# Queries, picks and group 0's scores of a fused attention kernel moved in among the last experts, the identity products of the attention groups taken out

## The chip, the cores and the metric

The kernel runs on one NeuronCore of a Trainium2 chip. The metric is device time in microseconds (us) of one execution, lower is better. The kernel before takes 216.92 us, the median of 3 runs (216.85 to 217.7).

## The reference

Input are `x` and a context, both 4 batches x 256 tokens x 128 features, in fp32. Two layers follow each other.

- Layer 0, attention: a normalised `x` against the context (similarities with softmax both ways), concatenated and sent through a linear layer, added to `x`.
- Layer 0, experts: after a second layer norm, `out = sum over 8 experts of weight[e] * ((silu(x W1[e]) * (x W2[e])) W3[e])`, hidden size 256, with the weights a softmax over the top 2 of 8 logits. All 8 experts are computed for all tokens; added to `x`.
- Layer 1, attention: third layer norm, then for 16 heads of size 8: `Q = x Wq`, `K = ctx Wk`, `V = ctx Wv`, `softmax(Q K^T / sqrt(8)) V`, then `Wo` and a bias; added to `x`.
- Layer 1, last product: fourth layer norm, values rounded to 8-bit floats, one 128x128 product, a bias, added to `x`.

## The kernel before, in words

Each engine has its own instruction stream, written out by hand in one `nc.Block`; there is no planner. An engine executes its stream in order, and semaphores (`S[...]`) tie the streams together. TensorE (`pe`) writes into eight PSUM banks `bk[0]` to `bk[7]`; ScalarE (`act`) and VectorE (`dve`) read them; GpSimd (`pool`) works on SBUF only. 1024 tokens are 8 tiles of 128, or two halves of 512.

**Start (to about 38.6 us).** First attention and values. `project_keys` (L1056) makes the keys of both halves in banks 2 and 3 after `turn("ln2", ...)`; ScalarE copies them over `ctxT` (L402), rounds them to `kx` (L488), and GpSimd makes the low part (L280).

**Experts.** 16 units `n`: half `n // 8`, expert `n % 8`. `up(n)` (L1084) makes four 128x512 results in banks 0 to 3, each of three products in a fast fp32 format (high and low parts, L933 to L935). ScalarE's `gates` (L404) applies silu, VectorE's `hidden` (L751) multiplies. `down(n - 2)` (L1101, products at L1110) follows `up(n)` on TensorE, into bank 4 or 5; VectorE's `weigh` (L760) adds the result times the expert's weight to `xs` (four instructions at L768). Once half 0 is done, at unit 9, VectorE takes the third norm's moments of it (`sum_moments`), GpSimd makes the deviation, ScalarE scales in units 10 and 11 (`third_scaled`), TensorE turns after `down(10)` in unit 12 (`turn("ln3", ..., 6, 0)`), projects the queries ahead of `up(13)`, and makes the picks of groups 0 and 1 ahead of `up(14)` and `up(15)`.

**Attention groups.** 16 groups `m`: batch `b = m // 4` and four heads `g = m % 4`. For a group:
- `pick_group` (L1120) lays queries and keys of four heads out on four quadrants of 32 rows by a selection matrix (bank 0 or 7), and ScalarE's `stacked` copies them to `stk`.
- `scores(m, r)`, r = 0 to 3 (L1132): one head each, 2 products; VectorE's `maxima` (L783, reduction at L789) takes the negated row maximum.
- `turn_maxima(m)` (L1149) turns the maxima, VectorE's `shifted` (L794) adds them to the queries as one more row (`qa`), and `shifted_scores(m)` (L1156, into banks 3 to 6) makes the shifted scores, of which ScalarE's `exps` (L442) are the probabilities.
- `outputs(m)` (L1170) multiplies with the values; `o_copy` saves them.
- After a batch: `turn_outputs(b, t)`, `normalise(b, t)` (VectorE, L802), `turn_normalised(b)`, ScalarE's copy, `output_layer(b)`, and `add_attention(b)` (VectorE, L812).

`pe_group(m)` (L1242) sets the order on TensorE: `turn_maxima(m)`; `bank7_used(m)` (the products for other batches that go through bank 7, and here the turn of the third norm's half 1 at m = 3 and the projection of its queries at m = 4); `scores(m+1, 1)`; `pick_group(m+3)`; `shifted_scores(m)`; `scores(m+1, 2)` and `(m+1, 3)`; `bank7_free(m)` (waits until bank 7 may be written); `outputs(m-1)`; `scores(m+2, 0)`. `keep_warm(bank, count)` (L945) multiplies the identity by itself `count` times; nothing reads the result. It appears 23 times between unit 15 and group 11 (each product is two records in the trace, L947). VectorE's order is in `dve_group` (L819), ScalarE's in `act_group` (L460).

**End.** After group 15's outputs: batch 3's turns, output layer, fourth norm, rounding, last product, in three chunks.

Of the kernel before, what the change touches and what calls it, by code (L numbers as in the profile page):

```python
# [33 lines left out]
WARMED = (0, 1, 2, 2 * G - 1, 3 * G - 1)  # L34
# [12 lines left out]
def build(nc, x_d, ctx_d, ctxT_d, small_d, wc_d, const_d, wl_d, bl_d, wg_d, w12_d, w3_d,  # L47
# [9 lines left out]
    with stack:  # L57
# [84 lines left out]
        x3T = sb("x3T", [P, TOK])  # L142
        qx = sb("qx", [P, 2, TOK], r32)
# [82 lines left out]
        def _(pool):  # L226
# [53 lines left out]
            pool.tensor_tensor(kx[:, 1, :], ctxT[:, :], plain(kx[:, 0, :]), ALU.subtract).then_inc(S["k_lo"], 1)  # L280
# [36 lines left out]
        def _(act):  # L317
# [78 lines left out]

            values_out(0)
            values_out(1)
            normed_hi(0)
            for h in range(2):  # L400
                act.wait_ge(S["k_ps"], h + 1)
                act.copy(ctxT[:, h * HALF:(h + 1) * HALF], bk[2 + h][:, :]).then_inc(S["k_out"], 1)  # L402
# [53 lines left out]
            def turned_out(b):  # L456
                act.wait_ge(S["aoT_ps"], b + 1)
                act.copy(aoT[:, :], bk[7][:, 0:SEQ]).then_inc(S["aoT_ev"], 1)

            def act_group(m):  # L460
# [5 lines left out]
                if m in TURNED_AT:  # L466
                    turned_out(b - 1)
                exps(m, 0)
                exps(m, 1)
                if m >= 1:  # L470
                    o_copy(m - 1, 0 if m == GROUPS - 1 else 7)
                if m + 3 < GROUPS:
                    stacked(m + 3)
                if m == 2:
                    for t in range(*HALVES[1]):
                        third_scaled(t)


            for n in range(UNITS):
                if n == 4:  # L480
                    logits_out(1)
                if n == UNITS - 3:
                    queries_hi(0)
                if n >= UNITS - 2:
                    stacked(n - UNITS + 2, 7)
                gates(n, n == 0)
                if n == 2:
                    act.copy(kx[:, 0, :], ctxT[:, :]).then_inc(S["k_hi"], 1)  # L488
# [13 lines left out]
            stacked(2)  # L502
# [53 lines left out]
        def _(dve):  # L556
# [203 lines left out]
            def weigh(n):  # L760
# [5 lines left out]
                for t in range(TPH):  # L766
                    tile = h * TPH + t
                    ins = dve.scalar_tensor_tensor(xs[:, tile, :], bk[4 + n % 2][:, t * P:(t + 1) * P],  # L768
# [43 lines left out]
            def add_attention(b, tiles):  # L812
# [3 lines left out]
                                  bk[7][:, 0:SEQ].rearrange("p (t d) -> p t d", t=TPB), ALU.add)\  # L816
                    .then_inc(S["x3_s"], 1)

            def dve_group(m):  # L819
# [5 lines left out]
                if more:  # L825
                    maxima(m + 1, 1)
                if m == G:
# [9 lines left out]
                if m in (0, 1):  # L837
                    sum_moments((TPH + TPB * m, TPH + TPB * (m + 1)))
                if b == BATCH - 1 and g == 1:
                    normalise(b - 1, 1)  # L840
                if more:
                    maxima(m + 1, 3)
                if m == GROUPS - 1:
                    moments(4, CHUNKS[0], lambda t: dve.wait_ge(S["x3_s"], t // TPB + 1))
                    add_attention(b - 1, slice(TPB * (b - 1), TPB * b))


            for n in range(UNITS):
# [7 lines left out]
                if n == UNITS - 3:  # L856
                    queries_lo(0)
                if n >= 2:
                    weigh(n - 2)
                if n == E + 1:  # L860
                    sum_moments(HALVES[0])
            weigh(UNITS - 2)
            dve.wait_ge(S["setup"], 1)
            maxima(0, 0, 1)
            weigh(UNITS - 1)
            maxima(0, 2, 3)
# [63 lines left out]
        def _(pe):  # L930
# [71 lines left out]
            context_to_query(1)  # L1002
            pe.wait_ge(S["cv_s"], 1)
# [52 lines left out]
            def project_keys(h):  # L1056
                if h == 0:
                    pe.wait_ge(S["aT_ev2"], BATCH - 1)
                ins = pe.matmul(bk[2 + h][:, :], wk[:, :], ctxT[:, h * HALF:(h + 1) * HALF], start=True, stop=True)
                ins.then_inc(S["k_ps"], 1)  # L1060

            for h in range(2):
                project_keys(h)
# [37 lines left out]
            def down(n):  # L1101
                e, p = n % E, n % 2
# [288 lines left out]
```

## Time and profile before

| | us |
|---|---|
| median of 3 runs | 216.92 |
| the profiled execution | 218.05 |
| its span (first to last instruction) | 216.3 |
| TensorE busy | 188.8 |
| VectorE busy | 139.3 |
| ScalarE busy | 103.9 |
| GpSimd busy | 36.7 |
| share of the chain that ended last: TensorE / VectorE / ScalarE | 74% / 11% / 5% |

The profile is one execution. Times in it are us from the span's start. PE is TensorE's products, PEld its weight loads, DVE VectorE, ACT ScalarE, POOL GpSimd. An fp32 product appears as two records. A product's end is modelled, and products are pipelined, so the step from one start to the next tells more than a duration. The granted clock is a share of 2.4 GHz; 0.50 is 1.2 GHz.

### The profile page before, as it was taken

The page shows a single profiled execution, that of the slowest core. Times are in us where ns is not written, and L with a number is a line of the kernel's source. Part 1 is how long each engine was busy: PE and PEld are TensorE (multiplying, and loading weights), DVE is VectorE, ACT ScalarE, POOL GpSimd, SP SyncE. Part 2 cuts the span into 40 slices and gives each one's busy share as a digit, 9 for nine tenths or more (in the row PEclk, how much of TensorE's full clock was granted, in tenths as well). Part 3 has the DMA queues.
Part 4 walks back from the last instruction along what each step waited for, and adds up shares of the span by engine and source line. Part 5 has one row for each costly group of instructions (what it writes and reads, how often), then busy time and mean ns, then how long its engine had stood idle before and what let it go on. Part 6 is the DMA issues. An engine that isn't in the chain of part 4 may idle for free.

```text
span 216.3 us, 3877 instructions
## 1 busy us (share of the span) xinstructions
PE 188.8 (87%) x1386; PEld 146.3 (68%) x1386; DVE 139.3 (64%) x404; ACT 103.9 (48%) x184; POOL 36.7 (17%) x52
## 2 busy tenths in 40 slices
PE   5599799999999999998999999799999998789221
PEld 4289498779798888996789886456666665554110
DVE  2559758666467647553546778477777876554684
ACT  2247467535422232533233146887577666345333
POOL 3623374624000000300000005200000000003400
PEclk9999999999999999999999999999999999655955
DMA  6992000000000000000000000000000000000002
GB/s 205 387 397 92 5 0 2 0 3 0 0 5 0 0 0 3 0 0 0 3 0 0 2 3 0 0 3 0 5 0 3 0 5 0 0 3 2 0 0 97
DMA packets 3330, 6.61 MB, mean 31 GB/s; under 512 B 880, under 2 KB 2160, under 8 KB 3056
## 3 DMA queue, kind: packets, MB, share of 16 engines
q1 hardware_dynamic: 1440, 5.51, 6.7%
q10 hardware_dynamic: 1872, 0.87, 1.4%
q8 instruction: 11, 0.18, 0.3%
q14 instruction: 7, 0.06, 0.1%
HBM read 5.84 MB, written 0.52 MB: 29 GB/s over the span
## 4 chain that ended last, share of the span: by engine, by line
PE 74%; DVE 11%; issue 5%; ACT 5%; ACTq 3%; POOL 1%; DVEq 0%
PE banks L1110 13%; PE bank L1144 9%; PE bank L1177 8%; PE bank L933 5%; PE bank L935 5%; PE bank L934 5%; DVE negm L789 4%; PE bank L947 3%; PE bank L1152 3%; PE banks L934 2%; PE banks L933 2%; PE banks L935 2%; ACTq L328 2%; PE bank L1186 2%; PE bank L1127 2%
## 5 line engine op out<-in xcount | busy, mean ns | idle before, releaser
L789 DVE TENSOR_REDUCE negm<-bank 128x2 f32<-128x512 f32 x64 | 43.0, 689 | 18.9 <-PE bank L1144 18.7
L446 ACT ACTIVATE raw<-banks 128x1024 f32<-128x1024 f32 x32 | 31.0, 1021 | 21.4 <-PE banks L1164 21.4
L409 ACT ACTIVATE att<-bank 128x512 f32<-128x512 f32 x32 | 19.1, 598 | 38.5 <-PE bank L935 25.6
L1144 PE MATMUL bank<-stk 32*128 32x256 f32 x128 | 29.9, 319 | 3.9 <-DVE negm L789 3.3
L1144 PEld LDWEIGHTS bank<-stk 32*128 32x128 f32 x128 | 19.4, 191 | 15.9 <-issue 12.8
L768 DVE SCALAR_TENSOR_TENSOR xs<-banks,rw,xs 128x128 f32<-128x128 f32 x64 | 18.0, 345 | 6.0 <-PE banks L1110 5.8
L1110 PEld LDWEIGHTS banks<-raw,attT 128*128 128x128 f32 x176 | 21.3, 191 | 0.9
L1110 PE MATMUL banks<-raw,attT 128*128 128x128 f32 x176 | 21.5, 275 | 0.0
L1177 PE MATMUL bank<-raw,vones 128*32 128x256 f32 x256 | 19.9, 433 | 1.1 <-DVE ao L808 1.0
L933 PE MATMUL bank<-xT,w 128*128 128x512 f32 x48 | 20.6, 428 | 0.0
L237 POOL TENSOR_SCALAR vpe<-mv 128x4 f32<-128x4 f32 (+1 forms) x9 | 2.4, 266 | 97.7 <-DVE mv L566 97.6
L935 PE MATMUL bank<-xT,w 128*128 128x512 f32 x48 | 18.8, 392 | 0.0
L934 PE MATMUL bank<-xT,w 128*128 128x512 f32 x48 | 18.8, 391 | 0.0
L438 ACT ACTIVATE stk<-bank,const 128x512 fp32r<-128x512 f32 x16 | 11.2, 699 | 8.8 <-PE bank L1127 8.8
L756 DVE TENSOR_TENSOR attT<-att,bank 128x512 f32<-128x512 f32 x11 | 7.5, 683 | 10.3 <-ACT att L409 10.3
L1164 PE MATMUL banks<-qa,stk 32*128 32x256 f32 x128 | 13.5, 335 | 0.5 <-DVE qa L798 0.5
L1177 PEld LDWEIGHTS bank<-raw,vones 128*32 128x32 f32 x256 | 8.4, 119 | 6.8 <-issue 1.9
L756 DVE TENSOR_TENSOR attT<-att,banks 128x512 f32<-128x512 f32 x11 | 7.6, 688 | 7.2 <-ACT att L409 7.2
L263 POOL TENSOR_TENSOR w<-raw,w 128x512 fp32r<-128x512 f32 x8 | 10.1, 1286 | 6.6 <-ACT w L341 5.2
L933 PEld LDWEIGHTS bank<-xT,w 128*128 128x128 f32 x48 | 9.0, 188 | 2.7 <-DVE xT L697 0.5
L1164 PEld LDWEIGHTS banks<-qa,stk 32*128 32x128 f32 x128 | 10.0, 198 | 0.9 <-DVE qa L798 0.9
L935 PEld LDWEIGHTS bank<-xT,w 128*128 128x128 f32 x48 | 9.0, 188 | 2.1
(194 smaller groups left out, 347.6 us busy)
## 6 DMA issues: line engine op xcount, KB each, us to landing
raw<-in_w SPq DMA_DIRECT2D x1, 2048.0 KB, 10.7
raw<-in_w SPq DMA_DIRECT2D x1, 1024.0 KB, 8.5
xs<-in_x SPq DMA_DIRECT2D x2, 256.0 KB, 3.2
ctxT<-in_ctxT SPq DMA_DIRECT2D x1, 512.0 KB, 5.3
ctx<-in_ctx SPq DMA_DIRECT2D x1, 512.0 KB, 7.4
wl<-in_wl SPq DMA_DIRECT2D x1, 256.0 KB, 7.6
picks<-in_sel ACTq DMA_DIRECT2D x1, 256.0 KB, 10.9
out<-cT SPq DMA_DIRECT2D x1, 256.0 KB, 2.1
```

What stands on the lines that cost most here:

```text
L409: act.activation(silus[:, k, :], bk[2 * k][:, :], ACT.Silu).then_inc(S["silu_s"], 1)
L446: act.activation(probs[:, m % 2, 2 * r:2 * r + 2, :, :].rearrange("p h k q -> p (h k q)"), pair[r][:, :], ACT.Exp, scale=ATT_SCALE).then_i ...
L756: dve.tensor_tensor(hid[n % 3][:, k, :], silus[:, k, :], bk[2 * k + 1][:, :], ALU.mult)\
L768: ins = dve.scalar_tensor_tensor(xs[:, tile, :], bk[4 + n % 2][:, t * P:(t + 1) * P], rw[:, tile, e:e + 1], xs[:, tile, :], ALU.mult, ALU.add)
L789: dve.tensor_reduce(negm[:, m % 2, :, c0:c0 + 1].rearrange("p t c -> p (t c)"), bk[score_bank(m, r)][:, :].rearrange("p (t k) -> p t k", t ...
L933: pe.matmul(out, w[0], x[0], start=start, stop=False)
L934: pe.matmul(out, w[0], x[1], start=False, stop=False)
L935: return pe.matmul(out, w[1], x[0], start=False, stop=stop)
L1110: ins = pe.matmul(bk[4 + p][:, rows], hid[n % 3][:, k, rows], w3raw[:, e, k * P:(k + 1) * P], start=t == 0 and k == 0, stop=t == TPH - 1 a ...
L1144: ins = pe.matmul(bk[score_bank(m, r)][:, t * SEQ:(t + 1) * SEQ], stk[rows, m % G, t * P:(t + 1) * P], stk[rows, m % G, SEQ:2 * SEQ], star ...
L1164: ins = pe.matmul(bk[3 + j][:, t * SEQ:(t + 1) * SEQ], stk[rows, g, SEQ + t * P:SEQ + (t + 1) * P], qa[rows, m % 2, :], start=True, stop=T ...
L1177: ins = pe.matmul(bk[bank][QUAD * j:QUAD * (j + 1), SEQ:2 * SEQ], vones[:, t, (m % G) * HPG + j, :], probs[:, m % 2, j, t, :], start=t == ...
```

## The change

- **Keys.** `project_keys(0)` moves up, to before the wait for `cv` (after `context_to_query(1)`), behind a wait for all attention DMAs; `project_keys(1)` stays after `turn("ln2", ...)`. ScalarE copies them to `kraw`, which is `x3T`'s memory, instead of `ctxT`, the first of them ahead of the values' copies.
- **Third norm, half 0, and queries.** All four scalings in unit 10, the turn in unit 11 after `up(11)`, the projection in unit 12 after `up(12)`, VectorE's `queries_lo` in unit 12.
- **Picks and group 0's scores.** Picks of groups 0, 1, 2 after `up(13)`, `up(14)`, `up(15)`; group 0's four scores around `down(12)` and `down(13)` in units 14 and 15, all through bank 6, and VectorE's reductions of them around `weigh(12)` and `weigh(13)`.
- **Last two downs.** `down(14)` goes to bank 0 after `scores(1, 0)`; `down(15)` goes to bank 7 inside group 0, after `shifted_scores(0)`. VectorE's `weigh(14)` and `weigh(15)` stand inside its group 0, each ahead of a reduction. `pick_group(3)` moves behind `scores(1, 2)`.
- **Third norm, half 1.** All four tiles' moments in group 1 (before: two in group 0, two in group 1); ScalarE's scalings ahead of `exps(2, ...)` (before: behind them).
- **Batch 2's outputs.** Both halves turned through bank 0: the first in group 13, the second at the end of group 13 (before: both at its start, one through bank 7, with `outputs(12)` waiting for both). `turn_normalised(2)` in group 14 and `output_layer(2)` at that group's end use bank 0. `add_attention(2)` moves from the end of VectorE's group 15 to the end of group 14. `outputs(14)` uses bank 7 and doesn't wait for `output_layer(2)`.
- **Identity products.** All 23 between unit 15 and group 11 go; four are added in group 15, behind `outputs(14)`. Those of the start stay.

The diff, cut to its core:

```diff
@@ placement of banks
         def score_bank(m, r):
             if m == 0:
-                return 2 - r % 2
+                return 6
...
         def turn_bank(b, t):
-            return 0 if t == 0 and b >= BATCH - 2 else 7
+            return 0 if b == BATCH - 2 or (t == 0 and b == BATCH - 1) else 7
+
+        def layer_bank(b):
+            return 0 if b == BATCH - 2 else 7
+
+        def y_bank(n):
+            return {UNITS - 2: 0, UNITS - 1: 7}.get(n, 4 + n % 2)
@@ ScalarE
+            keys_out(0)
             values_out(0)
             values_out(1)
             normed_hi(0)
...
+            keys_out(1)
...
+                if m == 2:
+                    for t in range(*HALVES[1]):
+                        third_scaled(t)
                 exps(m, 0)
                 exps(m, 1)
...
-                if m == 2:
-                    for t in range(*HALVES[1]):
-                        third_scaled(t)
...
-                if n == UNITS - 3:
+                gates(n, n == 0)
+                if n == UNITS - 4:
                     queries_hi(0)
-                if n >= UNITS - 2:
-                    stacked(n - UNITS + 2, 7)
-                gates(n, n == 0)
+                if n >= UNITS - 3:
+                    stacked(n - UNITS + 3, 7)
...
-                if n in (E + 2, E + 3):
-                    for k in range(HB):
-                        third_scaled(HB * (n - E - 2) + k)
-                if n == E + 4:
+                if n == E + 2:
+                    for t in range(*HALVES[0]):
+                        third_scaled(t)
+                if n == E + 3:
                     third_turned(0, TPH, 6, 0)
@@ VectorE, dve_group and units
                 if more:
                     maxima(m + 1, 1)
+                if m == 0:
+                    weigh(UNITS - 2)
...
                 if more:
                     maxima(m + 1, 2)
-                if m in (0, 1):
-                    sum_moments((TPH + TPB * m, TPH + TPB * (m + 1)))
+                if m == 0:
+                    weigh(UNITS - 1)
+                if m == 1:
+                    sum_moments(HALVES[1])
+                if more:
+                    maxima(m + 1, 3)
                 if b == BATCH - 1 and g == 1:
                     normalise(b - 1, 1)
-                if more:
-                    maxima(m + 1, 3)
+                if m == GROUPS - 2:
+                    add_attention(b - 1, slice(TPB * (b - 1), TPB * b))
...
+                if n >= UNITS - 2:
+                    maxima(0, 2 * (n - UNITS + 2))
                 if n >= 2:
                     weigh(n - 2)
+                if n >= UNITS - 2:
+                    maxima(0, 2 * (n - UNITS + 2) + 1)
@@ TensorE
+            pe.wait_ge(S["ld_att"], 7 * 16)
+            project_keys(0)
             pe.wait_ge(S["cv_s"], 1)
...
-                if m in WARMED:
-                    keep_warm(7, 2)
...
             def bank7_free(m):
                 b, g = m // G, m % G
+                if m == 1:
+                    pe.wait_ge(S["y_w"], UNITS)
...
-                if b >= 1 and g == 1:
-                    pe.wait_ge(S["ao_s"], TPB * (b - 1) + (1 if b < BATCH - 1 else TPB))
+                if 1 <= b < BATCH - 1 and g == 1:
+                    pe.wait_ge(S["ao_s"], TPB * (b - 1) + 1)
...
-                if m + 3 < GROUPS:
+                if 0 < m < GROUPS - 3:
                     pick_group(m + 3)
                 shifted_scores(m)
-                if final:
-                    pe.wait_ge(S["o_ev"], m - 1)
-                    output_layer(BATCH - 2)
-                    outputs(m - 1, 0)
+                if m == 0:
+                    down(UNITS - 1)
                 if more:
                     scores(m + 1, 2)
                     if m == 0:
-                        keep_warm(7, 2)
+                        pick_group(3)
                     scores(m + 1, 3)
-                if m == 0:
-                    keep_warm(7, 4)
-                if m >= 1 and not final:
+                if m >= 1:
                     bank7_free(m)
                     outputs(m - 1)
                 if m + 2 < GROUPS:
                     scores(m + 2, 0)
+                if m == 3 * G + 1:
+                    pe.wait_ge(S["ao_s"], TPB * (BATCH - 2) + 1)
+                    turn_outputs(BATCH - 2, 1)
+                if m == 3 * G + 2:
+                    pe.wait_ge(S["aoT_ev"], BATCH - 1)
+                    output_layer(BATCH - 2)
+                if final:
+                    keep_warm(2, 4)
...
-                if n == UNITS - 3:
-                    pe.wait_ge(S["route_s"], 18)
-                    project_queries(0)
-                if n == UNITS - 2:
-                    pe.wait_ge(S["pick_s"], 1)
-                    pe.wait_ge(S["k_lo"], 1)
-                if n >= UNITS - 2:
-                    pick_group(n - UNITS + 2, 7)
                 up(n)
...
+                if n == UNITS - 5:
+                    turn("ln3", "x3T_ps", 6, 0)
+                if n == UNITS - 4:
+                    pe.wait_ge(S["route_s"], 18)
+                    project_queries(0)
+                if n == UNITS - 3:
+                    pe.wait_ge(S["pick_s"], 1)
+                    pe.wait_ge(S["k_lo"], 1)
+                if n >= UNITS - 3:
+                    pick_group(n - UNITS + 3, 7)
+                if n >= UNITS - 2:
+                    scores(0, 2 * (n - UNITS + 2))
                 down(n - 2)
...
+                if n >= UNITS - 2:
+                    scores(0, 2 * (n - UNITS + 2) + 1)
+            pe.wait_ge(S["hid_s"], HB * UNITS)
+            scores(1, 0)
             down(UNITS - 2)
-            pe.wait_ge(S["hid_s"], HB * UNITS)
-            for r in range(2):
-                scores(0, r)
-            down(UNITS - 1)
-            pick_group(2)
-            scores(0, 2)
-            pe.wait_ge(S["stack_s"], 2)
-            keep_warm(7, 4)
-            scores(0, 3)
-            keep_warm(7, 3)
-            scores(1, 0)
```

## Rows read from the trace of the kernel before

**Rows 1.** The page, granted TensorE clock in 40 slices, in tenths.

```profile
PEclk9999999999999999999999999999999999655955
```

**Rows 2.** Windows: stretch, length, busy us (records) by engine, clock, DMA share, GB/s.

```profile
113.53:127.87 14.34, 14.28 (x115) 12.43 (x113) 10.26 (x27) 5.29 (x7) 0.00 (x0) 1.00 0.01 2
127.87:142.02 14.15, 12.47 (x128) 8.28 (x127) 9.64 (x19) 9.88 (x16) 4.28 (x6) 1.00 0.00 1
...
180.15:186.65 6.50, 4.50 (x44) 2.88 (x43) 3.82 (x9) 3.01 (x5) 0.22 (x1) 0.92 0.00 0
186.65:199.21 12.56, 11.24 (x81) 6.16 (x81) 6.81 (x24) 5.42 (x9) 2.29 (x4) 0.50 0.01 2
```

**Rows 3.** Timeline: start, us, instruction [idle before]; turn_maxima of groups 1, 3, 12 to 15.

```profile
127.87 0.44 PE L1152 MATMUL bank<-const,negm 128*128 128x128 f32 x2
...
136.15 0.44 PE L1152 MATMUL bank<-const,negm 128*128 128x128 f32 x2
...
176.01 0.44 PE L1152 MATMUL bank<-const,negm 128*128 128x128 f32 x2
...
180.15 0.44 PE L1152 MATMUL bank<-const,negm 128*128 128x128 f32 x2
...
186.65 0.69 PE L1152 MATMUL bank<-const,negm 128*128 128x128 f32 x2
...
191.94 0.69 PE L1152 MATMUL bank<-const,negm 128*128 128x128 f32 x2
```

**Rows 4.** Timeline: the wait for cv, and the start of unit 0.

```profile
23.98 0.31 PEld L1005 LDWEIGHTS banks<-const,cv 128*4 128x4 f32 x4 [1.71 <-DVE cv L638]
...
38.64 0.19 PEld L933 LDWEIGHTS bank<-xT,w 128*128 128x128 f32 x1 [0.51 <-DVE xT L697]
```

**Rows 5.** Timeline of TensorE: turns, projection, first pick, and down(13).

```profile
97.14 0.60 PE L941 MATMUL banks<-const,xn 128*128 128x128 f32 x4
98.50 1.10 PE L1117 MATMUL bank<-x3T,wq 128*128 128x512 f32 x2 [0.77 <-ACT x3T L427]
...
104.61 0.47 PE L1127 MATMUL bank<-qx,pick 32*128 32x256 f32 x2 [0.46 <-DVE qx L779]
...
113.53 1.95 PE L1110 MATMUL banks<-raw,attT 128*128 128x128 f32 x16
```

**Rows 6.** Chain that ended last: start, us, what; down(15), identity products, scores.

```profile
117.69 1.98 PE banks L1110 x16
...
120.58 1.09 PE bank L947 x8
121.67 0.43 PE bank L1144 x2
```

**Rows 7.** Groups by line: count | busy, mean ns | idle before.

```profile
L789 DVE TENSOR_REDUCE negm<-bank 128x2 f32<-128x512 f32 x64 | 43.0, 689 | 18.9 <-PE bank L1144 18.7
...
L768 DVE SCALAR_TENSOR_TENSOR xs<-banks,rw,xs 128x128 f32<-128x128 f32 x64 | 18.0, 345 | 6.0 <-PE banks L1110 5.8
```

**Rows 8.** Timeline: third norm of half 1, and the scores behind its turn.

```profile
133.26 0.20 POOL L276 TENSOR_TENSOR nmr<-nmr,rstd 128x4 f32<-128x4 f32 x1
...
137.49 1.38 PE L941 MATMUL bank<-const,xn 128*128 128x128 f32 x4 [0.90 <-ACT xn L413]
...
138.79 0.38 PE L1144 MATMUL bank<-stk 32*128 32x256 f32 x1
```

**Rows 9.** Timeline: outputs of group 12, of groups 14 and 15, last turns.

```profile
184.80 1.19 PE L1177 MATMUL bank<-raw,vones 128*32 128x256 f32 x16 [1.02 <-DVE ao L808]
...
195.03 3.66 PE L1177 MATMUL bank<-raw,vones 128*32 128x256 f32 x32
...
199.21 1.13 PE L1186 MATMUL bank<-const,heads_out 128*128 128x128 f32 x8 [0.52 <-ACT heads_out L454]
```

**Rows 10.** Windows, columns as in rows 2: two stretches of 3.40 us.

```profile
134.90:138.30 3.40, 2.45 (x23) 1.21 (x15) 1.67 (x4) 3.40 (x8) 0.00 (x0) 1.00 0.00 0
182.20:185.60 3.40, 1.75 (x30) 1.07 (x26) 2.80 (x7) 1.94 (x2) 0.00 (x0) 1.00 0.00 0
```

More of the change, by code:

```diff
@@ L142, in build @@
         x3T = sb("x3T", [P, TOK])
+        kraw = x3T
         qx = sb("qx", [P, 2, TOK], r32)
@@ L395, in normed_hi, with keys_out @@
                 act.copy(xT[:, 0, h * HALF:(h + 1) * HALF], bk[4 + h][:, :]).then_inc(S["xT_hi"], 1)
+            def keys_out(h):
+                act.wait_ge(S["k_ps"], h + 1)
+                act.copy(kraw[:, h * HALF:(h + 1) * HALF], bk[2 + h][:, :]).then_inc(S["k_out"], 1)
+            keys_out(0)
             values_out(0)
@@ L399, in _ @@
             normed_hi(0)
-            for h in range(2):
-                act.wait_ge(S["k_ps"], h + 1)
-                act.copy(ctxT[:, h * HALF:(h + 1) * HALF], bk[2 + h][:, :]).then_inc(S["k_out"], 1)
+            keys_out(1)
             def gates(n, first):
@@ L457, in turned_out @@
                 act.wait_ge(S["aoT_ps"], b + 1)
-                act.copy(aoT[:, :], bk[7][:, 0:SEQ]).then_inc(S["aoT_ev"], 1)
+                act.copy(aoT[:, :], bk[layer_bank(b)][:, 0:SEQ]).then_inc(S["aoT_ev"], 1)
             def act_group(m):
@@ L855, in _ @@
                     routing(n // 5)
-                if n == UNITS - 3:
+                if n == UNITS - 4:
                     queries_lo(0)
+                if n == UNITS - 2:
+                    dve.wait_ge(S["setup"], 1)
+                if n >= UNITS - 2:
+                    maxima(0, 2 * (n - UNITS + 2))
                 if n >= 2:
                     weigh(n - 2)
+                if n >= UNITS - 2:
+                    maxima(0, 2 * (n - UNITS + 2) + 1)
                 if n == E + 1:
                     sum_moments(HALVES[0])
[L862 to L866, printed above, removed]
             for m in range(GROUPS):
@@ L1002, in _, with project_keys @@
             context_to_query(1)
+            def project_keys(h):
+                ins = pe.matmul(bk[2 + h][:, :], wk[:, :], ctxT[:, h * HALF:(h + 1) * HALF], start=True, stop=True)
+                ins.then_inc(S["k_ps"], 1)
+            pe.wait_ge(S["ld_att"], 7 * 16)
+            project_keys(0)
             pe.wait_ge(S["cv_s"], 1)
@@ L1054, in _ @@
             turn("ln2", "xT_ps", 4, 0)
[L1056 to L1063, printed above, removed]
+            project_keys(1)
             def logits(h):
@@ L1109, in down @@
                     for k in range(HB):
-                        ins = pe.matmul(bk[4 + p][:, rows], hid[n % 3][:, k, rows], w3raw[:, e, k * P:(k + 1) * P],
+                        ins = pe.matmul(bk[y_bank(n)][:, rows], hid[n % 3][:, k, rows], w3raw[:, e, k * P:(k + 1) * P],
                                         start=t == 0 and k == 0, stop=t == TPH - 1 and k == HB - 1)
@@ L1123, in pick_group @@
                 pe.wait_ge(S["stack_s"], m)
+                if m == 3:
+                    pe.wait_ge(S["y_w"], UNITS - 1)
                 cols, rows = slice(b * SEQ, (b + 1) * SEQ), slice(g * QUAD, (g + 1) * QUAD)
@@ L1133, in scores @@
                 pe.wait_ge(S["stack_s"], m + 1)
-                if r == 0 and m > 0:
+                if m == 0:
+                    pe.wait_ge(S["s1_max"], r)
+                elif r == 0:
                     pe.wait_ge(S["s1_max"], 4 * m - 1)
-                elif r == 2 and m > 0:
+                elif r == 2:
                     pe.wait_ge(S["qa_s"], m)
-                elif r == 3 or (r == 1 and m > 0):
+                else:
                     pe.wait_ge(S["s1_max"], 4 * m + (r + 1) // 2)
-                elif r == 2:
-                    pe.wait_ge(S["s1_max"], 1)
                 rows = slice(QUAD * r, QUAD * (r + 1))
@@ L1157, in shifted_scores @@
                 pe.wait_ge(S["qa_s"], m + 1)
+                if m == 0:
+                    pe.wait_ge(S["y_w"], UNITS - 2)
                 g = m % G
@@ L1192, in turn_normalised @@
                 for t in range(TPB):
-                    ins = pe.transpose(bk[7][:, t * P:(t + 1) * P], ao[:, t, :], ident)
+                    ins = pe.transpose(bk[layer_bank(b)][:, t * P:(t + 1) * P], ao[:, t, :], ident)
                 ins.then_inc(S["aoT_ps"], 1)
```

40 lines of the change are left out of this document (18 added, 22 removed).

## The prediction

> **What bounds the kernel now.** The page's chain and its slices come first. TensorE carries most of the chain (74% of the span on the page), and it runs at 2.4 GHz (granted clock 9 of 10 or more) until slice 34, falls to 1.2 GHz (5) for two slices and again at the very end [rows 1]. So instructions on TensorE's path are what counts, and waits in its queue. The stretches [rows 2] show where it isn't dense: from 127.87 to 142.02 it is busy 12.47 of 14.15 us, in group 13 (180.15 to 186.65) 4.50 of 6.50, and from 186.65 to 199.21 it works at 1.2 GHz. Then I read the rows of the places that the diff touches: the start, units 12 to 15, groups 0 to 3, groups 13 to 15.
>
> I write T(m) for the start of group m's `turn_maxima`; before, T(1) is 127.87, and a regular group takes 4.14 (176.01 to 180.15) [rows 3]. I lay the new order out instruction by instruction in this profile's times.
>
> **Keys earlier, at the start: 0.** `project_keys(0)` goes into TensorE's wait for `cv` (1.71 us idle before 23.98), and it takes about 0.9. Its new wait is for all 7 attention DMAs, behind which `cv`'s products and all that follow are queued; nearly no DMA moves after slice 3, so it should be met. Unit 0 starts when VectorE has written `xT` (0.51 us idle before 38.64) [rows 4], and neither the values nor the norm ahead of it move, so the second key product isn't on the path before nor after. ScalarE's first key copy falls where it waits for the values. Bounds: -0.5 (that idle) to +1 (should the DMAs be late); I take 0.
>
> **Units 11 to 15.** Turn, projection, picks of groups 0 and 1 are still issued before unit 15's last up product, one unit earlier each. What goes is two waits: TensorE idles from 97.59 to 98.50 for the copy of x3T (the four turns end 0.45 after 97.14) and from 103.99 to 104.61 for q's low part [rows 5], together 1.53. Now each product has a whole unit (4.5 us) between it and its use. On ScalarE the four scalings of group 0's norm come together, 1.65 to 1.75, in a gap of about 3 between two units' gates; VectorE's `queries_lo` delays `weigh(10)` by 0.7, which has over 2 of slack. Added before the end of up(15) are scores(0,0) and (0,1), 0.43 each [rows 6]. So `down(13)` could start at 113.53 - 1.53 + 0.86 = 112.86; but pick(2) (0.66) and scores(0,2) (0.43) now stand ahead of it.
>
> **From there to T(1).** TensorE: pick(2), scores(0,2), down(13) 1.78, scores(0,3), scores(1,0), down(14), 5.5 in all (a down of 16 products is 1.98 with the gap behind it, 1.78 where nothing stands between, scores 0.43 [rows 6]), so T(0) = 118.4. VectorE keeps up: its reductions (0.69) and weighings (four of 345 ns, overlapped to 1.13 together) [rows 7] end with maxima(0,3) at 117.75. Then turn 0.45, scores(1,1), VectorE's qa from about 118.95 to 119.36, shifted scores to 120.05, down(15) to 121.85, scores(1,2) to 122.28. Here VectorE becomes the bound: maxima(1,2) 122.4 to 123.1, weigh(15) to 124.2, maxima(1,3) to 124.9, and `turn_maxima(1)` waits for the last. TensorE has pick(3), scores(1,3), scores(2,0) until 123.8 and stands 1.25. T(1) = 125.05, gain 2.8. Of the 15 identity products (30 records) in this stretch, 4.1 us at 1.09 for four [rows 6], and the 1.53 of idle, only half comes back: the scores beside the experts had cheap cover for their reductions, but two weighings have moved behind. Bounds: 1.25 less if the weighing's wait is doubled, 4.1 if it is hidden: 1.5 to 4.1.
>
> **Groups 1 to 3.** All four tiles' moments now stand in group 1, 1.1 us instead of about 0.65, before maxima(2,3), so T(2) comes 4.45 after T(1), not 4.13: -0.3, and T(2) = 129.5. The deviation then takes GpSimd 2.13 (moments' end to nmr at 133.46), ready at 130.8. The scalings move ahead of exps(2): 130.85 to 132.5, exps(2) to 134.45 (0.8 later than it could), the heads' copy to 134.8. In group 3 the turn into bank 7 waits for that copy, 0.8 idle, but then finds its four tiles ready, 0.45, where it now waits 0.90 and is paced by ScalarE to 138.79 (1.38 busy from 137.49) [rows 8]. T(3) to scores(4,1) shrinks from 2.64 (136.15 [rows 3] to 138.79) to 1.7: +0.9. Bounds: 0 (exps(2) on the path by its whole 1.65) to 1.35.
>
> **Identity products in groups 7 and 11.** They stand between turn_maxima and scores(m+1,1), which has to wait for VectorE's reduction (0.69) anyway, so they are nearly covered: those groups take 4.34 and 4.32 against 4.14, and I take 0.4 for both (bounds 0 and 1.1, their whole length). Those of groups 0 to 2 are in the sum above or covered likewise. T(13) = 180.15 - 2.8 + 0.3 - 0.9 - 0.4 = 176.35.
>
> **Group 13.** Now it takes 6.50, since outputs(12) at 184.80 waits for both halves of `normalise(2)`, through bank 7 (1.02 idle before it) [rows 9]. After, turns and normalised values use bank 0, outputs(12) waits for nothing of theirs, and the second half is turned after scores(15,0). Added up: to the first turn 0.8, turn 0.53, scores(14,1) and its reduction to 2.55, scores(14,3) to 3.15, outputs 1.05, scores 0.43, second turn 0.45: T(14) = T(13) + 5.05, gain 1.45. The price is in group 14: maxima(15,0) is behind normalise(2,1) on VectorE, so scores(15,1) starts at +1.55, not +0.95, and the output layer (0.45) comes before T(15); 4.9 in all at full clock, against 5.29 now at half (186.65 to 191.94): gain 0.4.
>
> **Group 15.** Before, from T(15) at 191.94 to the last turns at 199.21 are 7.27: output layer, and 32 records of outputs in 3.66 at 1.2 GHz, started late [rows 9]. After: turn 0.44, qa by +1.05, shifted scores to +1.7, exps 1.94 to +3.8; outputs(14) and four identity products lie beside the exps; outputs(15) 1.1, copy 0.4: +5.5, gain 1.8. VectorE and GpSimd end chunk 0's norm at about +5.2, so they're just in time. From 199.21 to the end (216.3) nothing changes: 17.1.
>
> **The clock.** It falls at 185.65, after TensorE was busy 1.75 of the 3.40 us before, and comes back at 199.3; the loosest stretch without a fall is busy 2.45 of 3.40 [rows 10]. The new group 13 is as dense as a regular one (outputs, scores, turns in a row), so I take it at 2.4 GHz throughout; the gain of groups 14 and 15 (2.2) hangs on that, and partly on outputs at 1.02 instead of 1.89. The products that go are real ones. By the Trainium skill (TensorE: Matmul & The Clock Gate, Part 4: PE-mode transpose) a transpose doesn't count as TensorE work in the same way; by that rule stretches of turns would look emptier once identity products are out, and the clock might fall there; that would be rival A or, if it lasts, C. The row of 134.90 to 138.30, half of it turns with no identity product in it and a clock of 1.00, speaks against.
>
> **Sum.** 2.8 - 0.3 + 0.9 + 0.4 + 1.45 + 0.4 + 1.8 = 7.45. Span 216.3 - 7.4 = 208.9. The profiled execution took 218.05, 1.75 more than its span, so 210.65 for one like it; the median of the runs shown (216.92) lies 1.13 below the profiled one, so **209.5**.
>
> **Rivals.**
> A: the new wait before turn_maxima(1) drops the clock. There TensorE would be busy about 2.1 of 3.40 us, between the two cases of [rows 10]. Were it low for the same 13.6 us as before, three groups would take up to 5.29 instead of 4.14: +3.5, 213.0. For: the gap of 1.25 itself. Against: down(15), dense, stands just ahead. 15%.
> B: the fall in the last groups stays. The order of group 13 gains its 1.45, but groups 14 and 15 run at 1.2 GHz and pay the added reduction wait as well: gain 2.8 - 0.3 + 0.9 + 0.4 + 1.45 - 0.9 = 4.35, 212.6. For: group 14 has two gaps of 0.3 to 0.5. Against: the long outputs between. 12%.
> C, the other side: without its identity products the group loop doesn't hold the clock at all; once low at group 1, it stays. Each group then costs 1.15 more, and with 14 of them the time is 209.5 + 16 = 225.5; from the seventh low group on the change is slower than before (7 times 1.15 is over 7.4). For: every identity product in the loop goes. Against: groups 3 to 6 and 8 to 10 have none now, and hold 1.00 [rows 1]. 6% slower, 3% near break-even.
> D: the change doesn't do what it says at the crossing: VectorE's weighings and reductions take back all that the identity products gave (T(1) gains 0.5, not 2.8), 211.8. 8%.
>
> **Chances.** The forecast 56% (its own range 208.0 to 211.2), A 15, B 12, D 8, C 9. Within 0.5% is about what a measurement here can tell from no change. Faster 0.91, same 0.03, slower 0.06. The range reaches below for a crossing at its better bound (1.3) and up over A: 207.5 to 213.6.
>
> **What would show it.** Right: an idle of 1 to 1.5 before turn_maxima(1), T(1) near 125; about 0.8 of idle before the turn of x3T in group 3; group 13 near 5; granted clock 1.00 up to the last outputs, and these in 1.0 to 1.1 for 16; no idle over 0.2 before picks and projections in units 11 to 15. Wrong: a clock of 0.50 in any group, a wait for the DMAs before `project_keys(0)`, T(1) later than 126.5, or VectorE later than TensorE in each group rather than at the crossing alone.

## The result, and the profile after

The changed kernel takes 229.16 us (median of 4 runs, 227.68 to 229.99), the kernel before 217.17 in the same comparison (4 runs, 216.85 to 217.7): 1.054 times as long, 95% interval 1.048 to 1.060. I had forecast 209.5. A kernel that may or may not lose TensorE's clock has runs far apart, so the medians below are over all runs, with the lowest and the highest beside them, while a ratio with an interval compares only the runs of each kernel within 1.5% of its fastest. The loss is one thing, TensorE's clock. Here are the page's slices (one digit for 5.6 us):

```profile
PEclk9889999999999999999999655555555599979655
```

It falls in slice 23 (6) and is at 5, 1.2 GHz, in the nine slices behind it; [rows 1] had 9 there. The windows of the changed kernel (columns as in [rows 2]) are the stretch up to the fall, the low stretch, and two regular groups after it:

```profile
121.80:125.20 3.40, 1.81 (x21) 1.39 (x20) 3.10 (x7) 0.50 (x1) 0.00 (x0) 1.00 0.01 2
127.82:179.20 51.38, 51.05 (x330) 32.80 (x329) 26.22 (x48) 26.37 (x40) 4.01 (x7) 0.50 0.00 1
183.68:191.96 8.28, 7.68 (x83) 5.26 (x82) 6.25 (x11) 6.17 (x10) 0.17 (x1) 1.00 0.01 3
```

In the 3.40 us before the fall TensorE is busy 1.81, as little as before the old kernel's fall (1.75, [rows 10]). Then it is busy 51.05 of 51.38 us and still the level doesn't come back before about 180.1. The starts of `turn_maxima` (timeline, L1169; they answer to [rows 3]):

```profile
122.90 0.44 PE L1169 MATMUL bank<-const,negm 128*128 128x128 f32 x2 [1.07 <-DVE negm L797]
...
127.82 0.69 PE L1169 MATMUL bank<-const,negm 128*128 128x128 f32 x2
...
153.87 0.69 PE L1169 MATMUL bank<-const,negm 128*128 128x128 f32 x2
...
160.31 0.69 PE L1169 MATMUL bank<-const,negm 128*128 128x128 f32 x2
...
187.82 0.44 PE L1169 MATMUL bank<-const,negm 128*128 128x128 f32 x2
...
191.96 0.44 PE L1169 MATMUL bank<-const,negm 128*128 128x128 f32 x2
...
197.04 0.38 PE L1169 MATMUL bank<-const,negm 128*128 128x128 f32 x2
...
202.97 0.64 PE L1169 MATMUL bank<-const,negm 128*128 128x128 f32 x2
```

The first of them is T(1), with the new wait of 1.07. A regular group at the low level takes 6.44 (153.87 to 160.31), at the high one 4.14 (187.82 to 191.96): 2.30 more each. From T(1) to T(13), 122.90 to 191.96, are 69.06; in the best variant below (experiment 10), which holds the clock there, the same stretch takes 51.07. So the long low stretch costs about 18.0. The start of the kernel looks as forecast: keys and then `cv`, unit 0 waiting for `xT`:

```profile
21.26 1.02 PE L1018 MATMUL bank<-ctxT,wk 128*128 128x512 f32 x2
22.74 0.31 PEld L1025 LDWEIGHTS banks<-const,cv 128*4 128x4 f32 x4 [1.28 <-DVE cv L646]
...
37.41 0.50 PE L947 MATMUL bank<-xT,w 128*128 128x512 f32 x1 [0.54 <-DVE xT L705]
```

All of that lies 1.2 us earlier than in the profile before, already ahead of the keys. From unit 0 to T(1) are 85.49 us, before 89.23 (38.64 in [rows 4] to 127.87).

### The profile page after: what moved, and what is told of

Its sections match the earlier page's. It is cut to its first block, busy times and chain, and to the rows that moved or that the text cites. A ratio compares the mean times of both kernels' runs of the same rounds, so it can differ in the third digit from the quotient of the medians.

```text
span 225.9 us, 3803 instructions
## 1 busy us (share of the span) xinstructions
PE 201.4 (89%) x1348; PEld 152.1 (67%) x1348; DVE 141.2 (63%) x404; ACT 104.2 (46%) x184; POOL 37.0 (16%) x52
## 4 chain that ended last, share of the span: by engine, by line
PE 75%; DVE 12%; issue 4%; ACT 4%; ACTq 3%; POOL 1%; DVEq 0%
PE bank L1161 12%; PE banks L1125 11%; PE bank L1196 10%; PE bank L947 5%; PE bank L949 5%; PE bank L948 5%; PE banks L1183 3%; PE bank L1169 3%; DVE negm L797 2%; PE bank L1205 2%; PE banks L947 2%; PE banks L948 2%; PE banks L949 2%; PE bank L1125 2%; PE bank L1218 2%
## 5 line engine op out<-in xcount | busy, mean ns | idle before, releaser
L797 DVE TENSOR_REDUCE negm<-bank 128x2 f32<-128x512 f32 x60 | 40.2, 689 | 31.7 <-PE bank L1161 31.6
L1161 PE MATMUL bank<-stk 32*128 32x256 f32 x120 | 35.2, 397 | 3.2 <-DVE negm L797 2.8
L1161 PEld LDWEIGHTS bank<-stk 32*128 32x128 f32 x120 | 24.1, 253 | 19.6 <-issue 18.8
L1196 PE MATMUL bank<-raw,vones 128*32 128x256 f32 x256 | 25.7, 534 | 0.0
L776 DVE SCALAR_TENSOR_TENSOR xs<-banks,rw,xs 128x128 f32<-128x128 f32 x56 | 15.8, 344 | 7.8 <-PE banks L1125 7.7
L1125 PEld LDWEIGHTS banks<-raw,attT 128*128 128x128 f32 x160 | 19.2, 192 | 1.2 <-issue 0.5
L1125 PE MATMUL banks<-raw,attT 128*128 128x128 f32 x160 | 19.7, 276 | 0.0
L1183 PE MATMUL banks<-qa,stk 32*128 32x256 f32 x128 | 17.3, 393 | 0.6 <-DVE qa L806 0.5
L1183 PEld LDWEIGHTS banks<-qa,stk 32*128 32x128 f32 x128 | 13.1, 242 | 1.2 <-DVE qa L806 1.2
L947 PEld LDWEIGHTS bank<-xT,w 128*128 128x128 f32 x48 | 9.0, 189 | 3.2 <-DVE xT L705 1.4
```

The costliest lines, as they stand in the source:

```text
L776: ins = dve.scalar_tensor_tensor(xs[:, tile, :], bk[y_bank(n)][:, t * P:(t + 1) * P], rw[:, tile, e:e + 1], xs[:, tile, :], ALU.mult, ALU.add)
L797: dve.tensor_reduce(negm[:, m % 2, :, c0:c0 + 1].rearrange("p t c -> p (t c)"), bk[score_bank(m, r)][:, :].rearrange("p (t k) -> p t k", t ...
L947: pe.matmul(out, w[0], x[0], start=start, stop=False)
L1125: ins = pe.matmul(bk[y_bank(n)][:, rows], hid[n % 3][:, k, rows], w3raw[:, e, k * P:(k + 1) * P], start=t == 0 and k == 0, stop=t == TPH - ...
L1161: ins = pe.matmul(bk[score_bank(m, r)][:, t * SEQ:(t + 1) * SEQ], stk[rows, m % G, t * P:(t + 1) * P], stk[rows, m % G, SEQ:2 * SEQ], star ...
L1183: ins = pe.matmul(bk[3 + j][:, t * SEQ:(t + 1) * SEQ], stk[rows, g, SEQ + t * P:SEQ + (t + 1) * P], qa[rows, m % 2, :], start=True, stop=T ...
```

## The experiments

Theory: the order is right, and the wait at the crossing into group 1 drops the clock, which the group loop then can't win back. Main rival: the loop needs the removed identity products everywhere. For each variant the three numbers are the lowest, the median and the highest time. Runs of the kernel before beside them had medians of 216.4 to 217.6.

**1. Four products in the crossing's wait.**

```diff
+                if m == 0:
+                    pe.wait_ge(S["p_s"], 2)
+                    keep_warm(3, 4)
                 if m + 2 < GROUPS:
                     scores(m + 2, 0)
```

Expected: 

> The changed kernel with four identity products (into bank 3, behind scores(1,3), after exps(0)) put into the idle of 1.07 us ahead of turn_maxima(1). Theory 1 (the wait at the crossing drops the clock, and the group loop then cannot win it back): the clock stays at 1.00 up to the last groups, T(1) does not move, and ten groups of 6.44 become 4.14 each: 23 us less than the changed kernel, 205 to 208. Theory 2 (the loop needs its identity products in every order): the clock still falls in groups 1 to 3, 226 to 230.

Measured: 210.56, 215.84, 228.4 (10 runs). Its profiled run (211.93) runs groups 5 to 12 at 4.14 to 4.15. The four products take about 1.1 us, and 0.42 of idle is left before `turn_maxima(1)`. They help, but not in each run: two of ten runs are at 226.9 and over, where the changed kernel has six of eight at 227.7 and over (four in the result, four in experiment 9). The profile shows shorter falls at about 130, 178 and 185, and one at 198.7 in the end part, where every profile here has one. The lowest time lies above the expected 205 to 208, since the ten low groups cost 18.0 and not 23. Theory 1 is right in kind, and too simple in that one wait was all.

**2. Transposes in their place.** `pe.transpose(bk[3][:, 0:P], ident, ident)`, four times.

Expected: 

> The same place, but four fp32 transposes of the identity instead of four products: same length, same idle covered. If only covered time counts (theory 1a), the clock holds as with products, 205 to 208. If transposes do not count as work (theory 1b, the rule of the Trainium skill, TensorE: Matmul & The Clock Gate, Part 4), it falls near 125 as in the changed kernel, 226 to 230.

Measured: 210.77, 223.18, 231.4 (4 runs, two of them at 230 and over, two at 216.3 and below). It tells nothing between 1a and 1b, for a reason that I had missed: the two fillers aren't of the same length. A transpose leaves one record and a product two. First the four transposes, then the four products of experiment 1:

```profile
121.17 0.66 PE L1283 MATMUL banks<-const 128*128 128x128 f32 x4
```

```profile
121.53 1.16 PE L961 MATMUL banks<-const 128*128 128x128 f32 x8
```

The transposes leave 0.92 of the wait open, the products 0.42. Transposes are taken up again in 10.

**3. The kernel before without its 23.**

Expected: 

> The kernel before with all 23 identity products between unit 15 and group 11 left out, and nothing else changed. Theory 1 (one wait of about 1 us with half-empty work around it): the old order then waits for VectorE in three pieces of 0.5 to 0.9 us at its own crossing, so a fall is likely there too, with 10 or more groups of 6.4: 230 to 240; if the clock holds, 216 to 217, and the new order of weighings and downs is the cause, not the missing products. Theory 2 says 230 to 240 without condition.

Measured: 221.77, 222.25, 231.35 (4 runs), 2.2% slower than before (interval 1.5% to 3.0%). That is neither of the two cases expected (230 to 240, or 216 to 217). In its profile the clock is low from 125.5 to 149.4, in the middle of group 4, and groups 5 to 12 take 4.14 without one identity product. So the removed products did hold the clock in the old order too, at the crossing, and the plain loop can hold it without them once it has it. It doesn't hold it always: in the profiles of this document groups 7 and 11, where the old order has two products each, are entered at the high level without them 13 times, and the clock falls there three times (at 184.1 in experiment 2, 178.5 and 172.8 in experiments 5 and 6).

**4. Products back at the group loop's places.** As 1, and two each in groups 0, 1, 2, 7, 11 ahead of `scores(m+1, 1)` into bank 7, two ahead of `scores(1, 3)`.

Expected: 

> The changed kernel with identity products put back in the group loop: two each in groups 0, 1, 2, 7, 11 ahead of scores(m+1,1), two ahead of scores(1,3) and four ahead of scores(2,0). Theory 1: clock holds as with four alone; the others are nearly covered by VectorE's reductions, so at most 1 us slower than the four alone: 205.5 to 209. Theory 2: this one holds and the kernel with four alone does not.

Measured: 209.68, 215.85, 225.2 (10 runs). No better than the four alone, and above the expected 205.5 to 209: theory 2 is out, and something is lost elsewhere. In its profile it is the last groups, low from 184.4 to about 192.

**5 and 6. Is it how long TensorE works or how much of it?** 16 products in a row in group 4, where the clock is low: on all 128 rows (the first added line), and on 32 (the loop in its place).

```diff
                 if m == G:
+                    keep_warm(7, 16)
...
+                    for _ in range(16):
+                        pe.matmul(bk[7][:, 0:P], ident[0:QUAD, :], ident[0:QUAD, :], start=True, stop=True, tile_position=(0, 0))
                     project_queries(1)
```

Expected (128 rows): 

> The changed kernel with 16 identity products (128 rows, 128 columns) in a row in group 4, ahead of the projection of the queries, where its clock is low. At 1.2 GHz they take 6.9 us. Theory W (what counts is how much of the array works, and the group loop with its 32-row and 32-column products does not win the level back though TensorE is busy all the time): the clock is back during or right after the burst, groups of 6.44 become 4.14 from there, some 6 of them: 229 + 6 - 14 = 221, and where the crossing holds by itself, 214. Theory R (the level comes back by chance of phase, not by density): no earlier return than group 9 to 11, 235.

Expected (32 rows): 

> The same place and count, but each product on 32 rows of the identity (32 rows, 128 columns): same records of busy time. Theory W: no return, 234 to 236 when low before it. If busy time alone counts: as the burst on 128 rows, 221.

Measured: 221.13, 222.83, 225.79 and 216.31, 227.03, 229.99 (4 runs each). The windows of the two profiles, first that with 128 rows (burst from 142.05), then that with 32 (from 143.07):

```profile
143.00:144.00 1.00, 1.00 (x7) 1.00 (x7) 0.00 (x0) 0.00 (x0) 0.00 (x0) 0.50 0.00 0
144.00:145.00 1.00, 1.00 (x9) 1.00 (x9) 0.00 (x0) 0.00 (x0) 0.00 (x0) 0.84 0.00 0
145.00:146.00 1.00, 1.00 (x11) 1.00 (x11) 0.00 (x0) 0.00 (x0) 0.00 (x0) 1.00 0.00 0
```

```profile
145.00:151.00 6.00, 6.00 (x26) 5.46 (x26) 0.00 (x0) 0.00 (x0) 0.00 (x0) 0.50 0.00 0
151.00:157.16 6.16, 6.14 (x38) 3.01 (x36) 2.48 (x4) 3.08 (x5) 0.40 (x1) 0.50 0.00 0
```

With 128 rows the high level is back about 2.3 us into the burst, and groups 5 to 10 then take 4.13 to 4.15. With 32 rows TensorE is busy without a gap for over 7 us (32 records in 7.19) and nothing comes back until 169.4. One profile alone would be weak: of seven other profiles that enter group 4 at the low level, without any burst, four come back in that group too (at 149.4 in experiment 3, at 143.3 in 8 and in its covered form in 9, at 144.4 with the transposes of 10), in or behind the projection of the queries, whose products have 128 rows; the changed kernel (twice) and the variant of experiment 2 don't. The times speak for the burst as well: had it brought nothing back, they should lie at 235 where the crossing loses the clock, and all four lie between 221.1 and 225.8. So theory W holds in this: busy time alone didn't win the level back, and a burst that differs from the first in its rows alone did not do what the first did. Columns weren't varied.

**7. Products in nearly every group.** As 4, with six ahead of `scores(2, 0)`, and two in groups 0 to 12 other than 3 and 4.

Expected: 

> The changed kernel with identity products at the group-loop places of the kernel before, but six instead of four ahead of scores(2,0), and two in every group from 0 to 12 other than 3 and 4. Theory 1 with W (falls come from loose stretches at a few places, and identity products among 32-row ones hold the level): fewer low runs than with the four places alone, nearly all runs in 209 to 213, at most 1.5 us dearer than the best runs so far (209.7), since most are covered by reductions. Theory 2b (the level is lost at group 13 to 15 and by chance, whatever stands in the groups): as wide as before it, 210 to 228.

Measured: 212.3, 215.78, 223.56 (6 runs): not "nearly all in 209 to 213". Each regular group took 4.48 instead of 4.14, so these two products are not covered everywhere, and the last groups lost the clock all the same. More products alone don't help; experiment 9 puts them elsewhere.

**8. The last groups' part alone**, on the kernel before.

Expected: 

> The kernel before with only the last groups' part of the change: batch 2's outputs through bank 0, its second turn at the end of group 13, outputs(12) without that wait, output layer at the end of group 14, four identity products in group 15. My sum for this part alone: group 13 from 6.50 to 5.05, group 14 from 5.29 to 4.9, from T(15) to the last turns from 7.27 to 5.5: 3.6 less, 213.3. If the clock falls there all the same (rival B): 1.45 less 0.9 paid back in group 14, 216 to 216.5. Should the order itself be no gain: 217.

Measured: 213.59, 215.43, 220.22 (6 runs), ratio 0.993 (0.986 to 1.000). In the profile (214.66) the last groups are at full clock throughout; T(13) to the last turns take 15.18, against 19.06 before. But the clock falls at 136.5, in group 3, which the variant leaves as it was, and is back at 143.3: groups 3 and 4 take 7.76 and 5.23, where the kernel before takes 5.87 and 4.56, so 2.6 of the 3.9 gained are lost again there.

**9. Covering the waits, four kernels on one chip.** The changed kernel once more; the changed kernel with variant 4's products and, over the waits left, these; group 13's wait alone, covered in the kernel before (`keep_warm(0, 5)` ahead of `outputs(12)`); and variant 8 with such cover.

```diff
+                if m == 3:
+                    pe.wait_ge(S["p_s"], 5)
+                    keep_warm(3, 3)
                 if m >= 2:
                     pe.wait_ge(S["o_ev"], m - 1)
+                if m in (3 * G + 1, 3 * G + 2):
+                    keep_warm(7, 2)
...
+                if m == GROUPS - 1:
+                    pe.wait_ge(S["o_ev"], m - 1)
+                    keep_warm(7, 3)
                 shifted_scores(m)
...
+                    if m in (3 * G + 1, 3 * G + 2):
+                        keep_warm(7, 2)
                     scores(m + 1, 3)
```

Expected (changed kernel again): 

> The changed kernel once more, beside its variants on one chip. Theory (the wait at the crossing drops the clock in nearly every execution): 226 to 230 in at least three of four runs; should it lie at 210 to 217 in several, the chip or the start of the run decides more than the wait, and the four products in the wait have done less than I think.

Expected (waits covered): 

> The changed kernel with the group-loop identity products of the earlier variant (two in groups 0, 1, 2, 7, 11, two ahead of scores(1,3), four ahead of scores(2,0)) and with products over the waits that are left: three ahead of the turn of x3T in group 3 (bank 3), two at the start of groups 13 and 14, two ahead of scores(14,3) and (15,3), three ahead of shifted_scores(15). Theory: each of these stretches is where the earlier variants lost the clock (130, 178 to 184, 198); with them covered most runs lie at 208 to 212, median 210, cost of the products under 0.7. Rival (a loop of 32-row and 32-column products is so near the edge that the clock is lost anywhere): as wide as before, 210 to 228, median 215.

Expected (group 13's wait, kernel before): 

> The kernel before with five identity products into bank 0 over group 13's wait ahead of outputs(12), nothing else. If the fall at 185.65 is due to that wait: the clock holds to the last outputs, 5 less for groups 14 and 15, 212 to 213, at 0.3 cost. If it falls a little later in group 14 all the same: 215.5 to 217.5.

Expected (variant 8, covered): 

> The kernel before with the last groups' part of the change and the same products over the waits of groups 3 (four, into bank 7), 13, 14 and 15. Theory: clock held to the last outputs, 213 with little spread (its own crossing is dense with identity products). Rival: same as the last groups' part alone, 213.6 to 220, median 215.4.

Measured: 213.46, 223.47, 229.83 (4 runs) | **208.85, 209.76, 210.74** (6) | 213.6, 215.6, 216.77 (12) | 212.9, 213.69, 215.09 (6). The changed kernel itself held the clock better here than in its first four runs, two of four; "at least three" was a miss. With all waits covered the spread of 10 to 20 us is gone in these six runs: 0.966 of before (0.962 to 0.969). The rival, as wide as before with a median of 215, didn't come. The cover of group 13's wait gave 0.993 (0.990 to 0.996), less than I expected, but its profiled run (213.6) shows the old last groups at full clock, which I use below. Variant 8 with cover has a third of the spread it had without (0.985 of before, 0.981 to 0.989), as expected; cover isn't certain, though: in its profile the clock still falls at 139.9, in group 3, behind four products and the turn of `x3T`.

**10. What kind of filler, and how much of it.** The best variant with every one of its products turned into a transpose; and without the products that stand inside the loop (groups 0, 1, 2, 7, 11 and ahead of `scores(1, 3)`), so that only those over long waits are left.

Expected (transposes): 

> The best variant so far (products over all waits of the changed kernel's group loop, 209.8), with every one of the products added or kept behind unit 15 replaced by an fp32 transpose of the identity of the same size into the same bank. If transposes hold the clock as products do: 208.8 to 211. By the rule of the Trainium skill (TensorE: Matmul & The Clock Gate, Part 4: PE-mode transpose) that a transpose does not count as work in the same way, the clock is lost at the crossing or in groups 3, 13, 14 in many runs: median 214 to 224, highest over 226.

Expected (long waits only): 

> The same variant without its products in groups 0, 1, 2, 7, 11 and ahead of scores(1,3); kept are those over the long waits: four ahead of scores(2,0), three in group 3, and those of groups 13 to 15. If only waits of about half a us and more have to be covered: 208.5 to 211, 0.3 to 0.5 below the variant with them (groups 7 and 11 take 4.14 instead of 4.37). If the loop's own products are needed too, the loss comes at 124 to 130 in some runs: median over 212, highest over 220.

Measured: 209.74, 211.84, 215.31 (6 runs) and **208.75, 209.97, 210.57** (6 runs), 0.970 of before (0.966 to 0.973). The page of the second, and its windows at the crossing and over the last groups:

```profile
PEclk9859999999999999999999999999999999999955
```

```profile
123.00:127.00 4.00, 3.06 (x34) 2.15 (x36) 3.70 (x10) 0.97 (x2) 0.00 (x0) 1.00 0.01 2
...
175.30:190.71 15.41, 14.51 (x154) 10.34 (x153) 10.50 (x33) 8.43 (x14) 2.58 (x5) 1.00 0.01 2
```

So the loop's own products could go, as the change has it; what had to stay or come is cover for the new waits. With transposes all six runs are better than before, but up to 5 us over the products. By the times alone that could be their length, since each covers little more than half of what a product does. The profile speaks against length alone: the clock is lost at 123.9 (and back at 144.4), right behind this stretch:

```profile
120.50:123.90 3.40, 3.05 (x21) 2.11 (x21) 2.72 (x7) 0.90 (x2) 0.00 (x0) 1.00 0.01 2
```

TensorE is busier there than in stretches of experiment 1 and of the second variant that kept the clock (2.45 of 3.40 from 122.20, 2.46 from 123.00). The rule of the Trainium skill (TensorE: Matmul & The Clock Gate, Part 4), that transposes do not count for the clock as products do, agrees with that one profile; the full loss that I had drawn from it (median 214 or more) did not come, and no run has transposes and products of equal length.

## Why the prediction was wrong

The step that failed is the clock's: "so I take it at 2.4 GHz throughout", and with it the 6% and 3% for rival C. All else in the order of work came out near, or better:

| term | forecast | measured |
|---|---|---|
| unit 0 to T(1) | 2.8 less | 3.74 less (changed kernel's profile) |
| T(1) to T(13) | 1.0 less | 1.21 less (long waits only: 51.07 against 52.28) |
| T(13) to last turns | 3.65 less | 3.65 less (15.41 against 19.06), all of it clock |
| wait before turn_maxima(1) | 1.25 | 1.07 |
| group 13 | 5.05 | 5.08 |
| time with the clock held | 209.5 | 209.8 and 210.0 (medians with products over the waits) |

That the last row agrees is partly luck: the terms of the last groups were wrong and met in the right sum (below), and it needs products that the change doesn't have.

**The crossing.** I had listed the wait as rival A, with the right place and nearly the right busy share (2.1 of 3.40 forecast, 1.81 measured), but at 15% and with a low stretch as long as the old kernel's 13.6 us. There the level came back right behind 32 records of outputs in a row (3.66 from 195.03 [rows 9]; 128 rows, 32 columns); in the loop nearly every product uses 32 rows or 32 columns, and at most 16 outputs stand in a row. I read "busy", and in the low stretch busy is 51.05 of 51.38. Experiments 5 and 6 show that rows make a difference. The rows that speak against C (groups without identity products at 1.00) show only that the loop keeps the level, not that it regains it. C is what happened, for about ten groups instead of all; what ends the stretch at 180.1 isn't shown (175.6 in the second profile of the changed kernel).

The comparison by busy share was weak from the start. The loosest stretch without a fall in the old profile isn't the one at 2.45 of 3.40: from 20.80 to 24.20, ahead of `cv`, TensorE is busy 2.09 of 3.40 and the clock stays at 1.00. And the stretch at 2.45 is no safe side: in experiment 8's profile the same instructions, busy 2.45 of 3.40 from 132.88, are followed by a fall at 136.5.

**The price of a low group** was 1.15 in the forecast, from group 14, which has no pick and is partly waits. A regular one costs 2.30. So C's point of turning was not the seventh low group but the fourth (7.45 / 2.30 = 3.2). Ten times 2.30 would be 23, but group 1 is low only at its end and group 10 only at its start, and group 3 takes 6.43 against 5.24: the stretch costs 18.0. A second fall at 200.6 costs 1.0 from T(13) to the last turns (16.41 against 15.41), and 209.5 + 18.0 + 1.0 = 228.5 is near the 229.16 measured.

**The removed products** were priced by their time alone, and the time was about right: in experiment 3, with nothing else changed, unit 0 to T(1) takes 87.31 instead of 89.23, and groups 7 and 11 take 4.14 instead of 4.35 and 4.36. Their effect on the clock stood in no term of the sum, and that experiment is 2.2% slower. An instruction that is nearly free in time need not be free to take out.

**The last groups.** My split was wrong. At full clock the old order takes 15.14 from T(13) to the last turns, the new one 15.41. (With no product over its waits the new order takes 15.18, in the two profiles where the clock held by itself.) The timeline of the kernel before with group 13's wait covered:

```profile
185.98 0.44 PE L1152 MATMUL bank<-const,negm 128*128 128x128 f32 x2
...
189.69 0.44 PE L1152 MATMUL bank<-const,negm 128*128 128x128 f32 x2
...
194.79 1.09 PE L1186 MATMUL bank<-const,heads_out 128*128 128x128 f32 x8 [0.52 <-ACT heads_out L454]
```

Group 14 takes 3.71 there against 5.07 in the new order: what the new order saves in group 13 (6.33 to 5.07) it gives back in 14, where I had compared with 5.29 at the low level. All 3.65 are the clock's, and the new order alone doesn't secure it: in seven of the nine profiles that have it with no product over its waits, the clock falls between T(13) and the last turns. With the clock held up to there in both orders the profiled times are 209.47 and 213.60, so the order of work itself is worth 4.1.

**What stays open.** The changed kernel lost the clock in all four first runs and in two of four on another occasion; what differs is not shown. Nor is it settled which waits the clock stands and which it doesn't: no run varied one wait alone in steps, and the same stretch kept and lost it in different profiles. It isn't shown either what brings the level back inside the loop after 44 to 55 us, or how much of the transposes' loss is their length.

## What to carry to other kernels

Before you take out products that nobody reads, or put a wait where the work around it is on a few rows or columns of TensorE, ask what it costs if the clock falls there, and for how long: read the period of your loop at both levels, and look in a trace how long a low stretch lasts in it. Cover the waits of half a us and more with products on all rows into a free bank (here 0.97 of the time before, and a spread of 2 us in place of 17); leave them out where a reduction's wait is short. If you swap one filler for another, compare how long each lasts. And judge such a kernel by all its runs.

## What the runs showed of the hardware

- At 1.2 GHz a loop mostly of 32-row and 32-column products ran 51.38 us, busy 51.05 by the profile, without the level coming back; in a burst of 16 fp32 products of 128 rows it was back after about 2.3 us, in one of 16 products of 32 rows, over 7 us long, it was not (one profile each).
- An fp32 transpose of 128x128 is one record, a product two: four take 0.66 us against 1.16. As many transposes as products over the waits gave 209.7 to 215.3 against 208.8 to 210.7, and the clock fell once behind a stretch busy 3.05 of 3.40.
- The same stretch of instructions, busy 2.45 of 3.40, was followed by a fall in one profile (136.5, experiment 8) and by none in another ([rows 10]).
- One fall cost about 18.0 us, and runs of one kernel on one chip lay between 213.5 and 229.8.
